# Second attention of a two-layer kernel: rows sent in halves of a group, places written before the scores of a coming group

## The reference, cut to what matters

```python
x = x + attention(layernorm(x), ctx, ctx, phi...)      # second attention
h = layernorm(x)                                       # the rows that go to the experts
top_v, top_i = top_k(h @ Wg.T, 2)                      # the choice
pos = cumsum(onehot(top_i)) - 1                        # place of each row within its expert
batches[expert, pos] = h                               # rows beyond a capacity are dropped
out = x + sum(gate * expert(batches))                  # experts: gelu(inp) * gate, then W2
```

## Time and profile before

| what | value |
|---|---|
| median of 3 runs | 886.07 us (883.26 to 892.51) |
| profiled execution, its own time | 890.67 us |
| its span, first to last instruction | 889.0 us |
| busy, share of the span | TensorE 79%, VectorE 62%, ScalarE 45%, GpSimd 34% |
| mean granted TensorE clock | 0.889 of full |

### The profile page before, as it was taken

One profiled execution on the slowest core, in us unless ns is written; L12 is line 12 of the kernel. 1 busy time (PEld: TensorE's weight loads), 2 busy tenths in 40 slices (PEclk: granted clock), 3 DMA queues, 4 the chain that ended last, 5 costly groups with the idle time before them and its releaser, 6 DMA issues.

```text
span 889.0 us, 19049 instructions
## 1 busy us (share of the span) xinstructions
PE 700.3 (79%) x6278; PEld 550.1 (62%) x6278; DVE 547.8 (62%) x1322; ACT 403.1 (45%) x720; POOL 302.8 (34%) x306
## 2 busy tenths in 40 slices
PE   5476796989564799999999899996862098898981
PEld 4232454555354688888897798895531087777771
DVE  7768576887836545647556656547696446566441
ACT  1135466576513434646545555442552044546331
POOL 7505301416337422222121131232167414334342
PEclk9689799989776799999999999997875599999996
DMA  4562300601524542536344643425022555464332
GB/s 140 118 141 51 59 2 24 180 24 49 153 81 151 185 129 36 165 51 171 78 126 98 170 112 101 107 39 179 25 101 95 174 170 131 115 147 114 63 55 40
DMA packets 68418, 92.24 MB, mean 104 GB/s; under 512 B 14442, under 2 KB 54435, under 8 KB 68348
## 3 DMA queue, kind: packets, MB, share of 16 engines
q1 hardware_dynamic: 41788, 63.37, 24.1%
q0 software_dynamic: 14592, 16.24, 10.6%
q10 hardware_dynamic: 11968, 11.72, 5.3%
HBM read 64.21 MB, written 29.87 MB: 106 GB/s over the span
## 4 chain that ended last, share of the span: by engine, by line
PE 48%; DVE 18%; issue 11%; ACT 9%; POOL 5%; DMA 5%; ACTq 2%; another core or an unknown queue 1%; DVEq 0%; POOLq 0%; SPq 0%
PE ps L685 45%; POOL rows L631 3%; DVE probs L1726 3%; DVE mx L1591 2%; DMA out_x<-keys,row_to 2%; DVE keys L1804 2%; DMA probs<-rows 2%; ACT probs L1189 1%; ACT probs L1271 1%; ACT expo L1186 1%; DVE keys L1783 1%; ACT probs L1267 1%; PE ps L933 1%; DVE stats L1383 1%; ACTq L1252 1%
## 5 line engine op out<-in xcount | busy, mean ns | idle before, releaser
L1804 DVE TENSOR_TENSOR keys<-probs,ps 128x512 f32<-128x512 f32 x122 | 82.8, 687 | 177.3 <-ACT probs L1267 86.3
L685 PE MATMUL ps<-keys,slot 128*128 128x256 f16 (+1 forms) x1440 | 146.5, 263 | 5.4 <-DVE keys L1783 2.7
L685 PE MATMUL ps<-keys,probs 128*128 128x256 f16 (+1 forms) x1488 | 139.5, 255 | 5.1 <-DVE probs L1405 3.7
L685 PEld LDWEIGHTS ps<-keys,slot 128*128 128x128 f16 x1440 | 127.8, 99 | 22.8 <-issue 5.4
L685 PEld LDWEIGHTS ps<-keys,probs 128*128 128x128 f16 x1488 | 124.2, 98 | 19.0 <-issue 7.2
L575 POOL DMA_INDIRECT attended<-keys,row_to x42 | 67.2, 1601 | 166.0 <-ACT keys L1280 142.2
L1267 ACT ACTIVATE probs<-ps 128x512 f32<-128x512 f32 x122 | 71.4, 598 | 65.9 <-PE ps L685 63.7
L1280 ACT ACTIVATE keys<-ps,carried 128x256 f32<-128x256 f32 x80 | 33.5, 470 | 117.9 <-POOLq L580 41.6
L1809 DVE TENSOR_TENSOR probs<-keys,probs 128x512 f16<-128x512 f32 x122 | 83.3, 688 | 3.6 <-ACT probs L1271 1.9
L1271 ACT CAST probs<-keys 128x512 f16<-128x512 f32 x122 | 74.8, 614 | 22.0 <-DVE keys L1804 21.9
L1726 DVE TENSOR_TENSOR probs<-expo,probs 128x512 f16<-128x512 f32 x80 | 61.1, 775 | 34.1 <-ACT probs L1189 28.2
(11 more groups left out here) (285 smaller groups left out, 1145.7 us busy)
## 6 DMA issues: line engine op xcount, KB each, us to landing
inbox<-in_W SPq DMA_DIRECT2D x24, 512.0 KB, 3.9
probs<-rows ACTq DMA_DIRECT2D x44, 260.0 KB
inbox<-in_wg SPq DMA_DIRECT2D x16, 512.0 KB, 5.2
inbox<-in_wu SPq DMA_DIRECT2D x16, 512.0 KB, 3.7
inbox<-in_wd SPq DMA_DIRECT2D x16, 512.0 KB, 4.2
rows<-zeros SPq DMA_DIRECT2D x16, 260.0 KB
x<-in_x SPq DMA_DIRECT2D x4, 512.0 KB, 6.1
q_out<-queries SPq DMA_DIRECT2D x8, 256.0 KB, 2.1
```

Of the source, the lines that this page charges most:

```text
L685: return pe.matmul(o, l, r, start=start, stop=stop, **kw)
L1804: dve.tensor_tensor(h32[:, j % 2, :], s_act[:, j % 2, :], ps[:, 2 * (j % 2) + 1, :], ALU.mult).then_inc(S(r + "_h32"), 1)
```

## The change

- `low_rows(g)`: two instructions of two tiles each in place of one of four, each with a signal `r1_xp` of its own, so eight signals in place of four.
- `tokens_normalised(g)` on ScalarE: two tiles are normalised and cast, then two more. `gates(g)` stands between the halves.
- `scatter` on GpSimd: for the second layer it waits for the first half of the rows ahead of the first DMA and for the second half ahead of the fifth; the wait for `r1_slot` stays ahead of all.
- VectorE's order: behind `gate_difference(g)` come `place(g)`, `low_rows(g)`, and `logits(g + 2)` last.

```diff
--- before.py
+++ after.py
@@ -622,9 +622,12 @@
 
             def scatter(l, g):
                 r = l.r
-                pool.wait_ge(S(r + "_xp"), g + 1)
+                if l.n == 0:
+                    pool.wait_ge(S(r + "_xp"), g + 1)
                 pool.wait_ge(S(r + "_slot"), g + 1)
                 for t in range(GT):
+                    if l.n == 1 and t % 2 == 0:
+                        pool.wait_ge(S(r + "_xp"), 2 * g + t // 2 + 1)
                     if l.n == 1 and t == 2 and g + 1 < NG:
                         scale_and_shift("r1", g + 1)
                     for k in range(TOP):
@@ -1339,11 +1342,15 @@
 
             def tokens_normalised(g):
 
-                if g:
-                    act.wait_ge(S("r1_xp"), g)
-                normalise("r1", g, g + 1)
-                act.wait_ge(S("r1_ln"), GT * (g + 1))
-                act.copy(xps[g][:, :, 0:D], xln[:, :, :]).then_inc(S("r1_xhi"), 1)
+                for j in range(2):
+                    if g:
+                        act.wait_ge(S("r1_xp"), 2 * g - 1 + j)
+                    half = slice(2 * j, 2 * j + 2)
+                    normalise("r1", g, g + 1, (2 * j, 2 * j + 1))
+                    act.wait_ge(S("r1_ln"), GT * g + 2 * j + 2)
+                    act.copy(xps[g][:, half, 0:D], xln[:, half, :]).then_inc(S("r1_xhi"), 1)
+                    if j == 0:
+                        gates(L[1], g)
 
             def coming_high_parts(e):
                 for n in range(len(L[1].chunks)):
@@ -1358,18 +1365,14 @@
             weights_turned(1)
             tokens_turned(3)
             tokens_normalised(0)
-            gates(L[1], 0)
             exponentials(2)
             weights_turned(2)
             coming_high_parts(1)
             tokens_normalised(1)
-            gates(L[1], 1)
             exponentials(3)
             weights_turned(3)
             tokens_normalised(2)
-            gates(L[1], 2)
             tokens_normalised(3)
-            gates(L[1], 3)
             experts(L[1])
 
 
@@ -1897,8 +1900,10 @@
 
             def low_rows(g):
 
-                dve.wait_ge(S("r1_xhi"), g + 1)
-                dve.tensor_tensor(xps[g][:, :, D:2 * D], xln[:, :, :], xps[g][:, :, 0:D], ALU.subtract).then_inc(S("r1_xp"), 1)
+                for j in range(2):
+                    half = slice(2 * j, 2 * j + 2)
+                    dve.wait_ge(S("r1_xhi"), 2 * g + j + 1)
+                    dve.tensor_tensor(xps[g][:, half, D:2 * D], xln[:, half, :], xps[g][:, half, 0:D], ALU.subtract).then_inc(S("r1_xp"), 1)
 
             weighed_value_parts()
             coming_low_parts(0)
@@ -1922,10 +1927,10 @@
                     low_weights(g + 1)
                 choose(L[1], g)
                 gate_difference(g)
+                place(L[1], g)
+                low_rows(g)
                 if g + 2 < NG:
                     logits(g + 2)
-                low_rows(g)
-                place(L[1], g)
             count(L[1])
             experts(L[1])
```

## The result

Twenty runs of each kernel gave a median of 889.23 us for the changed one (886.39 to 894.47) and 883.73 us for the one before: ratio 1.006, 95% interval 1.0045 to 1.0075. The forecast's 895.3 us also stood on a median of three runs that was 2.3 us above the median of twenty, so the two are compared as differences and not as times. The profiled execution took 891.34 us, its span is 889.6 us.

The account below looks back on a forecast made before the run. GpSimd's DMA queue was taken as the bound; late start, idle queue at scalings (1.2 and 5 us), group 1's start and small remainders made +9.2 us on 886.07, so 895.3; own range 893 to 897, wide range 887 to 901.

Parts of the forecast that it names:

- The scores of group 2: VectorE's `logits(2)`, moved behind places and low rows of group 0: done at 652.03 instead of 645.48, 6.55 us later.
- the first DMA: GpSimd's first DMA of group 0 needs the first half of the rows: 649.92 instead of 649.32, 0.6 us later.
- the first scaling: GpSimd's scaling in the middle of group 0 waits for VectorE's moments of group 1: 1.2 us idle.
- the second: GpSimd's scaling in the middle of group 1 waits for the moments of group 2: 5 us idle.
- the rival of the slow clock: TensorE stays at 1.2 GHz through scores and weighing of group 2: 3.2 us more, 898.5 us; chance 0.14.
- The third rival: Not slower: GpSimd's queue stays the bound and runs through the scalings of groups 0 and 1; 884.0 us, chance 0.07.
- The third scaling: GpSimd's last scaling, in group 2: moments of group 3 are ready at 689.1, before 691.2, so no wait.
- The start of group 1: First DMA of group 1, behind late scores, slow weights and weighing: 667.05 instead of 663.28, 3.8 us later.
- One of these DMAs meets them. Such a meeting cost 0.9 us: End of group 1: a GpSimd DMA runs beside VectorE's low halves of group 2 and takes 0.9 us more.
- Group 3 and what follows keep their length.: GpSimd's queue from group 3 on, started 9.2 us later, takes as long as before.
- The line of 1%: About 8.9 us over the kernel before, at 894.9 us: what a measurement can tell from no change.
- the 0.52 for "slower": Chance of landing above the 1% line: 0.38 from the main case plus 0.14 from the clock rival.

Follow-up runs that it names:

- e1: Changed kernel with VectorE's old order back (scores, low halves, places) and the halves kept; ratio 0.998 to the kernel before.
- e9: Changed kernel with scores ahead of places and low halves, and three last low parts of weights made in six instructions of 512 columns; one execution, no ratio.
- e2: Changed kernel's new VectorE order, but with the low rows whole instead of in halves; ratio 1.006 to the kernel before.
- e8: Changed kernel with the scores ahead of places and low rows, and the rows whole; ratio 0.9986 to the kernel before.
- e6: Changed kernel plus 56 unread matmuls on TensorE behind the positions of group 0; ratio 1.0092 to the kernel before.
- e6b: Changed kernel plus 116 unread matmuls on TensorE behind the positions of group 0; ratio 1.0068 to the kernel before.

## Why the prediction was right and wrong

Right, by the profile after, each step in the record's own terms:
- The bound is GpSimd's queue. One reading for it was wrong: most of the 28.3% of "issue" is not the 0.30 us between two DMAs, since 28 such gaps are 8.4 us of 22.6. The waits bear the conclusion without it.
- As forecast, `place(0)` gains nothing by its new place, since the positions release it. The places began 0.04 us behind the positions.
- The scores of group 2 come 6.3 us later behind the anchor (6.55 forecast), the first DMA 0.33 (0.6), the first scaling waits 1.57 (1.2), the second 5.60 (5).
- TensorE turned the weights at 1.2 GHz and was back at 2.4 inside the scores, so the rival of the slow clock did not come. Group 1 started 2.9 us later (3.8).
- The third rival, a queue that runs through, asked for no wait at the scalings; they waited 1.57 and 5.60 us.
- The third scaling waits for nothing, and what follows group 3 keeps its order.

Wrong in size: +9.2 was forecast, the queue shows +6.55 and the timed ratio +5.3. What failed is the sum of the queue's delay, and its 2.7 us too many (64.1 against 61.37 in the table) are three terms that were mis-sized; the largest is the price of a meeting.
- *The start of group 1*, 0.83 us: the positions came 16.52 us behind the anchor, 0.55 earlier than in the record, and VectorE followed them after 0.03 us, not 0.3.
- *"One of these DMAs meets them. Such a meeting cost 0.9 us"*, and the same once more in group 2's second part. The first meeting cost 1.44 - 0.97 = 0.47 (the wait ahead of it was 0.5 us longer than in the sum, so at the start of group 2 the forecast is 1.07 us off, only 0.24 more than at that of group 1), the second 0.03: the DMA at 690.61 took 1.00 though the low halves of group 3 ran from 690.08 to 691.43. From the start of group 2 to that of group 3 the queue took 12.90 us; 13.9 were in the sum, 13.79 it was before. The two meetings are 1.3 us of the sum. Here the halves do what the record denied them: they open a gap in which a DMA gets through.
- *"Group 3 and what follows keep their length."* The table of blocks, and with it VectorE's low parts, came later against the queue; a DMA had just started at 695.75, and one DMA was held (1.98 at 697.03) where two were before (1.61 and 1.96). 9.97 us in place of 10.59, so 0.62 less.

The remaining 1.2 us between the queue and the timed ratio is within the interval. The record set the row's 0.9 above what it worked out from the Trainium skill, "SBUF — State Buffer", section "SBUF: two separate sides", where whichever instruction starts first has the shared port pair for its whole length. The runs agree with that in one direction: a DMA that starts beside a low half ends 0.86 us behind that half's end (679.99 for 679.13), where it takes 0.97 alone, and the next half does not hold it further. The other direction no run shows: in e1 a low half took its usual 0.68 us at 657.83, though a DMA had started at 657.42 and took 0.97. The 0.9 was what a whole instruction cost that began 0.2 us ahead of the DMA; a half, or another distance, costs something else, so each meeting has to be worked out from the two starts.

The line of 1% lay at 894.9 and the forecast at 895.3, so the 0.52 for "slower" hung on 0.4 us. All three terms were taken too costly, and each alone would have put the forecast below the line.

## What to carry to other kernels

Work that stands ahead of a wait may cost nothing there, because the engine would stand idle anyway: before moving it behind the wait, look at who hangs on that work two steps on, and not at the instruction alone. Compare two profiles from an event ahead of the change, as the start of the changed stretch wanders by more than the change is worth. Idle time of the bound engine is not a sum of prizes: 4 us taken away at one wait gave 0.8, since the same late work held the next wait.

## What the runs showed of the hardware that was not expected

An indirect DMA on GpSimd takes 0.97 to 0.99 us if no long VectorE instruction with two inputs from SBUF runs when it starts (1.11 for the very first, 1.09 for the one behind a scaling). If one does, the DMA ends 0.84 to 0.86 us behind the end of that one instruction: 661.70 for 660.86 before, 679.99 for 679.13 in the changed kernel (the second half, 677.85 + 1.28), 691.85 for 691.00 in e9. An instruction that follows on VectorE does not hold it further. One with an input from PSUM does not hold it at all: the DMA of 653.31 took 0.98 beside the low weights of 653.05 to 653.72. In these profiles a meeting with the low rows cost 0 to 0.5 us where they came in halves, and 0.7 to 0.9 where they came whole (before, e2, e8).

TensorE stayed at 1.2 GHz through the whole weighing of group 3 at 669.97, 6.23 us without a pause, in the changed kernel as in the one before, while 3.9 us of scores raised it in the same profile. In e9 it even fell inside the weighing of group 2, which was without a pause: granted clock 1.00 from 649.96 to 651, 0.58 in the next us, 0.50 behind it. Fill of 3.3 us was lost again after 4.1 us without work (e6); fill up to 0.74 us ahead of the next matmul held it (e6b).
